# Order of the score and maxima units in an attention round, grouped maxima, scalar-tensor-tensor forms

## The reference

```
q, k, v = split_heads(xn @ Wq), ...        # 16 heads of 64
q, k = rope(q), rope(k)                    # the first 32 dimensions of a head
sim  = einsum('bhid,bhjd->bhij', q, k) / 8
out  = (softmax(sim) @ v) @ Wout + bout
ffn  = fp4_linear(silu(fp4_linear(xn, w_gate)) * fp4_linear(xn, w_up), w_down)
```

## Time and profile before

| | us |
|---|---|
| median of 3 runs (2223.3 to 2225.09) | 2224.7 |
| the profiled execution's own time | 2221.72 |
| its span | 2219.8 |
| TensorE busy | 1910.8 (86%) |
| VectorE busy | 1721.6 (78%) |
| GpSimd busy | 1492.2 (67%) |
| ScalarE busy | 813.5 (37%) |
| mean granted TensorE clock | 0.955 |

### The profile page before, as it was taken

The page is one execution under the profiler, slowest core; times in us unless marked ns, Lnnn a source line. Parts: engine busy times, 40 slices in busy tenths (PEclk is TensorE's granted clock), DMA queues, the critical chain, the costliest instruction groups (busy, mean ns, idle before and its releaser), DMA issues. The chain is left out here.

```text
span 2219.8 us, 30955 instructions
## 1 busy us (share of the span) xinstructions
PE 1910.8 (86%) x11492; PEld 1201.5 (54%) x11492; DVE 1721.6 (78%) x2251; ACT 813.5 (37%) x1012; POOL 1492.2 (67%) x691
## 2 busy tenths in 40 slices
PE   1377788658999999999999999999999999999779
PEld 0266678634555555555555555555555555555379
DVE  8799999748787778888787777888778777888144
ACT  1111112103444444444444444444444444444332
POOL 2355545316877887888887787888877778788700
PEclk8589989869999999999999999999999999999889
DMA  8000110130111120111112111111221111100175
GB/s 289 37 29 29 40 43 33 37 104 29 25 40 43 30 82 30 44 30 42 42 39 79 33 44 30 42 32 40 63 59 35 39 43 31 30 25 25 39 275 185
DMA packets 128057, 125.58 MB, mean 57 GB/s; under 512 B 40752, under 2 KB 92592, under 8 KB 127792
## 3 DMA queue, kind: packets, MB, share of 16 engines
q1 hardware_dynamic: 127920, 123.77, 17.9%
HBM read 83.36 MB, written 40.37 MB: 56 GB/s over the span
## 5 line engine op out<-in xcount | busy, mean ns | idle before, releaser
L1070 POOL TENSOR_TENSOR acc<-acc,prob 128x1024 f32<-128x1024 f32 x384 | 947.9, 2469 | 223.6 <-ACT prob L1113 198.2
L955 DVE TENSOR_REDUCE half_max<-m_ps 128x2 f32<-128x1024 f32 x512 | 623.5, 1218 | 322.3 <-PE m_ps L829 319.2
L1113 ACT ACTIVATE prob<-s_ps 128x1024 f32<-128x1024 f32 x512 | 500.1, 1025 | 425.3 <-PE s_ps L853 423.3
L868 PE MATMUL o_ps<-prob,v 128*64 128x512 f32 x2048 | 492.6, 602 | 0.0
L829 PE MATMUL m_ps<-k_hi,q_hi 64*128 64x512 f32 x1024 | 239.0, 463 | 61.8 <-DVE half_max L955 58.3
L868 PEld LDWEIGHTS o_ps<-prob,v 128*64 128x64 f32 x2048 | 130.0, 136 | 244.7 <-issue 179.2
L1052 POOL TENSOR_TENSOR turned<-straight,shuffled 128x512 f32<-128x512 f32 x128 | 179.1, 1399 | 95.2 <-DVE shuffled L987 95.2
L898 PE MATMUL misc_ps<-xT,wqk 128*128 128x512 f32 x768 | 219.8, 423 | 17.7 <-DMA xT<-xn_scratch 10.2
L898 PEld LDWEIGHTS misc_ps<-xT,wqk 128*128 128x128 f32 x768 | 139.0, 194 | 143.1 <-issue 108.2
L1070 POOL TENSOR_TENSOR acc<-prob 128x1024 f32<-128x1024 f32 x64 | 168.2, 2629 | 60.2 <-ACT prob L1113 60.2
L853 PE MATMUL s_ps<-max_rows,ones_r 64*128 64x512 f32 x1024 | 202.9, 393 | 0.0
(11 more groups left out here) (126 smaller groups left out, 2421.9 us busy)
## 6 DMA issues: line engine op xcount, KB each, us to landing
wqk<-wp_scratch SPq DMA_DIRECT2D x32, 512.0 KB, 4.4
inv_rows<-inv_scratch SPq DMA_DIRECT2D x128, 128.0 KB, 2.9
o_scratch<-o_norm SPq DMA_DIRECT2D x64, 256.0 KB, 2.0
o_in<-o_scratch SPq DMA_DIRECT2D x8, 2048.0 KB, 9.8
xn_scratch<-xnT SPq DMA_DIRECT2D x8, 1024.0 KB, 4.3
xT<-xn_scratch SPq DMA_DIRECT2D x8, 1024.0 KB, 6.6
wv<-wp_scratch SPq DMA_DIRECT2D x32, 256.0 KB, 3.5
wp_scratch<-wp_hl SPq DMA_DIRECT2D x8, 768.0 KB, 3.9
```

The costliest lines, as they stand in the source:

```text
L868: ins = nc.tensor.matmul(o_ps[head * DH:(head + 1) * DH, :], v[s // 2 % 2][:, kt, s % 2, at:at + DH], prob[n % SLOTS][:, head, :], start=k ...
L955: nc.vector.tensor_reduce(half_max[:, t % 2, part, :], m_ps[:, :, :], axis=AX.X, op=ALU.max, negate=True).then_inc(half_maxed, 1)
L1070: nc.gpsimd.tensor_tensor(acc[b][:, :, :], first, prob[n % SLOTS][:, :, :], ALU.add).then_inc(added, 1)
L1113: nc.scalar.activation(prob[n % SLOTS][:, :, :], s_ps[n % 2][:, :, :], ACT.Exp).then_inc(exp_done, 1)
```

## The change

In every round of the attention TensorE's order becomes score unit, guess, score unit, guess (it was guess, score unit, score unit, guess). The value units go ahead of the column sums (they were behind them). `half_max` becomes larger and `combine` runs once for four query tiles instead of once for each, with a scalar-tensor-tensor in place of a tensor-tensor; what waits for `max_done` counts halves now. `normalise` becomes a scalar-tensor-tensor of the same operands. The orders of the other engines and of the jobs in `misc_ps` stay.

```diff
-    half_max = sb("half_max", [P, 2, 2, 2], F32)
+    half_max = sb("half_max", [P, 2, 2, 2, GRP], F32)
...
-                pe.wait_ge(max_done, s * QT + 4 * half + 4)
+                pe.wait_ge(max_done, 2 * s + half + 1)
...
             for s in range(-2, STEPS + 1):
                 for r in range(ROUNDS):
+                    if scoring(s):
+                        scores(s, 2 * r)
                     if scoring(s + 1):
                         guess(s + 1, 2 * r)
                     if scoring(s):
-                        scores(s, 2 * r)
                         scores(s, 2 * r + 1)
                     if scoring(s + 1):
                         guess(s + 1, 2 * r + 1)
+                    for n in (s * UNITS + 2 * r - 2, s * UNITS + 2 * r - 1):
+                        if 0 <= n < STEPS * UNITS:
+                            values(n)
                     if r == 2 and scoring(s - 1):
                         column_sums(s - 1, 1)
                     if r == 6 and scoring(s):
                         column_sums(s, 0)
-                    for n in (s * UNITS + 2 * r - 2, s * UNITS + 2 * r - 1):
-                        if 0 <= n < STEPS * UNITS:
-                            values(n)
...
-                t, part = divmod(s * UNITS + i, 2)
-                if t >= 2:
-
-                    dve.wait_ge(max_done, t - 1)
-                nc.vector.tensor_reduce(half_max[:, t % 2, part, :], m_ps[:, :, :], axis=AX.X, op=ALU.max,
+                t, part = divmod(i, 2)
+                half = 2 * s + t // GRP
+                if half >= 2:
+
+                    dve.wait_ge(max_done, half - 1)
+                nc.vector.tensor_reduce(half_max[:, half % 2, part, :, t % GRP], m_ps[:, :, :], axis=AX.X, op=ALU.max,
                                         negate=True).then_inc(half_maxed, 1)
 
-            def combine(s, t):
-
-                dve.wait_ge(half_maxed, s * UNITS + 2 * t + 2)
-                cols = max_cols[t // 4][:, :].rearrange("p (h n) -> p h n", h=2)[:, :, t % 4]
-                nc.vector.tensor_tensor(cols, half_max[:, t % 2, 0, :], half_max[:, t % 2, 1, :], ALU.min).then_inc(max_done, 1)
+            def combine(s, half):
+
+                dve.wait_ge(half_maxed, s * UNITS + (half + 1) * QT)
+                cols = max_cols[half][:, :].rearrange("p (h n) -> p h n", h=2)[:, :, 0:GRP]
+                nc.vector.scalar_tensor_tensor(out=cols, in0=half_max[:, half, 0, :, :], scalar=1.0, in1=half_max[:, half, 1, :, :],
+                                               op0=ALU.mult, op1=ALU.min).then_inc(max_done, 1)
...
-                nc.vector.tensor_tensor(o_norm[b][:, :], o_raw[b][:, :], inv_rows[b][:, :], ALU.mult).then_inc(normed, 1)
+                nc.vector.scalar_tensor_tensor(out=o_norm[b][:, :], in0=o_raw[b][:, :], scalar=1.0, in1=inv_rows[b][:, :],
+                                               op0=ALU.mult, op1=ALU.mult).then_inc(normed, 1)
...
-                        combine(s + 1, r)
+                        if r in (3, 7):
+                            combine(s + 1, r // 4)
```

## The result

The changed kernel takes 2375.05 us in the median (2369.23 to 2378.18), the kernel before 2224.3 us beside it: a ratio of 1.0675, 95% interval 1.0653 to 1.0696. The forecast was 2338 us in a range of 2306 to 2378, slower at 0.95: direction and range held, but the middle lies 37 us low.

A forecast was written before the change was run, and what follows sets the result against it. TensorE's own instruction order was taken to set the pace. Terms 159 - 68 - 29 + 51 = +113 us on the profiled 2221.7 gave 2335, and 2338 us for the median, range 2306 to 2378.

The forecast's parts named there:

- Two guesses on one `m_ps`: In every round with guesses and scores, the second guess waits for the first's reduction: 0.64 us, 248 times, +159 us.
- the sum: The prediction's added terms; per step, 46.9 us without waits + 8 x 0.64 + 2 x 0.86 = 53.7 us, against 50.16.
- The old guess waits go: TensorE's three waits a step before guesses, for VectorE's reduction, would vanish: 31 x 2.2 us, -68 us.
- Sums behind the values: Rounds 2 and 6: the next projection waits for ScalarE's copy of the column sums, 59 x 0.86 us, +51 us.
- the wait for `straight`: Column sums in rounds 2 and 6 wait for the evacuation of `misc_ps`; predicted to go, 59 x 0.50 us, -29 us.
- The two terms: At the column sums: -29 us for the vanished evacuation wait, +51 us for the projection waiting on ScalarE's copy.
- The vector forms: On VectorE, grouped `combine` and scalar-tensor-tensor `normalise`: `o_norm` takes 0.68 us, lateness removed; +0 beyond the -68 us already counted.
- Not late: Round 3 into 4: VectorE finishes at T + 4.4 us after the second guess at T, before the next guess at T + 4.9.
- the third rival: VectorE's new forms stay as slow as before beside GpSimd: up to 1.3 us a step, about +20 us, 2358 us; chance 8%.
- The clock rival: TensorE's granted clock falls to 0.93 during the steps because it idles more: +109 us, about 2447 us; chance 7%.

## Why the prediction was right, and where it fell short

- **Two guesses on one `m_ps`: right.** 1.71 us from guess to guess was worked out, 1.72 measured; 0.54 of idle, 0.56 measured; 248 places, 247 in the list. With a value unit between the guesses the wait goes in seven of eight rounds. The order alone gives 4.75 us a step and 2370 us, though, where the sum had 8 x 0.64 - 2.2 = 2.9: 1.2 of the rest is round 4, 0.5 the longer wait for `straight`.
- **The old guess waits go: right in two of three places, and in the largest by luck.** The account was that VectorE would no longer be late, with 0.68 for `o_norm`. The 1.34 us in round 0, behind the `o_norm` of round 7, did go, but that `o_norm` still takes 2.89: the leading score unit and the longer round cover it. The 0.40 behind the turn of round 4 went too. The small one, 0.29 in round 4 behind the `o_norm` of round 3 (1.77 before), came back as 1.19 us on top of the 0.56.
- **Sums behind the values: right.** A stall of 0.86 forecast, 0.81 measured (1.72 less the 0.91 of the sums), and the wait for `straight` gone. The two terms came to +22 us; alone, the edit costs 0.54 us a step and 13 us, and beside the new order, which had made the wait for `straight` longer, 5 us with the vector forms, within the intervals of the two runs.
- **The vector forms: this step failed.** "So the new `o_norm` (same shape, both inputs in SBUF) should take 0.68" was wrong, and with it "Not late" for the first guess of round 4: in round 3 `o_norm` or the `k_lo` ahead of it takes 2.9, and VectorE is free 6.6 us behind the second guess of round 3 (1320.39 - 1313.75), where the prediction had 4.4. Its worth is (54.95 - 53.75) = 1.2 us a step, some 37 us, the distance between the forecast and the result. With the reads of GpSimd's additions taken away the step is 53.75 us for 53.7 forecast, so this is the whole of the difference in the steps. The evidence that I took for it, 64 `q_lo` of 0.68 us beside a busy GpSimd, was an effect of the order: each had a `combine` right ahead that had already done the waiting. This is the third rival, which had 8%; its upper bound, 1.3 us a step, is what came, and not the half that I took.
- The sentence of the Trainium skill (SBUF — State Buffer, Who interferes with whom), that VectorE with two SBUF inputs contends with a GpSimd instruction that reads SBUF, holds for the scalar-tensor-tensor too: 2.88 us beside additions, 0.68 beside a memset. I set it aside for a row whose neighbours I had not looked at.
- **The clock rival** did not come: the granted clock is 1.00 over the 28 steps, and lower at the start only.
- **Wrong in the experiments:** that a value unit can be put between the guesses for nothing, and that all the old guess waits descend from `o_norm` alone.

## What to carry to other kernels

With a single buffer between two engines, work out the round trip (here 0.43 to the reader, 1.23 of reading, 0.05 back) and count what lies between two uses; a reordering that takes this cover below the round trip adds what is missing each time. A job that is moved behind its wait may lose the cover of the wait behind it: with one unit on either side both were hidden. And a row that shows an instruction undisturbed proves little until one has looked at what stands ahead of it on its engine.

## What the runs showed of the hardware

- A VectorE instruction with two SBUF inputs waits for the GpSimd addition under way, in the tensor-tensor form and in the scalar-tensor-tensor form alike (2.88 us for 0.68), and does not wait for a memset (0.68).
- One that follows directly behind an instruction that had waited may get in before GpSimd's next one, which then is 0.5 us longer (2.95 and 2.84 for 2.37). In the kernel before 120 `low` were of this kind, and all took 0.68 to 0.69; in the changed kernel `k_lo` behind `combine` was short in 18 steps and 2.96 us in 12, though in all 30 `k_lo` and GpSimd's next addition start within 0.02 us of each other; what decides between them stays open.
- Where value units (matmuls on 64 columns of the array) and guesses or scores (64 rows) follow each other, TensorE's starts lie some 0.1 us further apart at each change: a value unit takes 1.02 before another kind and 0.93 before its like; a guess takes 0.42 with value units on either side, 0.32 with a score unit ahead and a value unit behind, 0.23 with score units on either side (1303.78 to 1304.01 in the changed kernel).
